# Layer 0: second products of two neighbouring routed tiles as one unit, four buffers for gated products, a new plan

## The reference

```python
def _swiglu(t, a, b, c):
    return jax.nn.silu(t @ a) * (t @ c) @ b
scores = jax.nn.softmax(xt @ gate_w.T, axis=-1)
topk_w, topk_i = jax.lax.top_k(scores, 2)
comb = jnp.zeros((T, E)).at[jnp.arange(T)[:, None], topk_i].add(topk_w)
for e in range(E):
    y = y + comb[:, e:e + 1] * _swiglu(xt, w1[e], w2[e], w3[e])
y + _swiglu(x, sw1, sw2, sw3)
```

## Time and profile before

| | us |
|---|---|
| median of 3 runs | 1134.03 |
| lowest and highest | 1131.99, 1137.25 |
| the profiled execution | 1132.48 |
| its span | 1130.3 |
| PE busy in it | 1026.9 |
| DVE busy | 869.8 |
| ACT busy | 730.9 |

### The profile page before, as it was taken

The page is one execution under the profiler, slowest core; times in us unless marked ns, Lnnn a source line. Parts: engine busy times, 40 slices in busy tenths (PEclk is TensorE's granted clock), DMA queues, the critical chain, the costliest instruction groups (busy, mean ns, idle before and its releaser), DMA issues.

```text
span 1130.3 us, 22735 instructions
## 1 busy us (share of the span) xinstructions
PE 1026.9 (91%) x8315; PEld 533.1 (47%) x8315; DVE 869.8 (77%) x1814; ACT 730.9 (65%) x1220; POOL 429.5 (38%) x484
## 2 busy tenths in 40 slices
PE   4589999889989999899889999899999889999996
PEld 2112222224555555446555566566565434455464
DVE  3799888898887888797557877777876688687455
ACT  4048766877767776666466566565657767767763
POOL 3000212354033346325135433453344468434463
PEclk9569988999999999999898999999999999999998
DMA  4804434356664777557548577695767846412110
GB/s 136 173 24 129 112 87 114 112 189 180 214 203 149 235 205 215 155 161 201 152 139 230 155 226 232 192 249 179 229 185 220 222 126 183 104 43 61 50 40 19
DMA packets 122510, 176.06 MB, mean 156 GB/s; under 512 B 20280, under 2 KB 86200, under 8 KB 122400
## 3 DMA queue, kind: packets, MB, share of 16 engines
q1 hardware_dynamic: 116064, 161.24, 49.1%
q0 software_dynamic: 5760, 12.59, 3.9%
q10 hardware_dynamic: 576, 0.79, 0.3%
HBM read 114.77 MB, written 59.67 MB: 154 GB/s over the span
## 4 chain that ended last, share of the span: by engine, by line
PE 46%; DVE 20%; DMA 15%; issue 8%; ACT 4%; POOL 3%; SPq 3%; POOLq 0%; DVEq 0%; ACTq 0%
DVE nm L965 12%; PE ps L775 10%; PE ps L837 8%; PE ps L758 5%; PE ps L736 5%; PE ps L856 5%; DMA gr<-d_y,pos 4%; PE ps L873 2%; PE ps L880 2%; DMA DR<-d_r 2%; ACT ES L1320 2%; DMA d_h<-r,pos 2%; PE ps L785 2%; DMA d_r<-DC 1%; PE ps L718 1%
## 5 line engine op out<-in xcount | busy, mean ns | idle before, releaser
L965 DVE TENSOR_REDUCE nm<-ps 128x2 f32<-128x1024 f32 (+3 forms) x512 | 507.7, 1016 | 103.5 <-PE ps L742 57.2
L1320 ACT ACTIVATE ES<-ps 128x1024 f32<-128x1024 f32 (+3 forms) x512 | 430.0, 862 | 160.3 <-PE ps L758 90.1
L775 PE MATMUL ps<-ES,VS 128*9 128x512 f32 (+3 forms) x2048 | 231.1, 528 | 0.8 <-DVE nmp L976 0.4
L736 PE MATMUL ps<-KS,QS 48*128 48x512 bf16 (+3 forms) x1024 | 183.8, 366 | 38.5 <-DVE nm L965 23.6
L758 PE MATMUL ps<-QS,KS 51*128 51x512 bf16 (+3 forms) x1024 | 178.0, 352 | 20.0 <-DVE nm L965 11.6
L837 PE MATMUL ps<-hsT,wst 128*128 128x128 f32 x1104 | 158.6, 288 | 3.7 <-DVE hdx L1158 3.4
L837 PEld LDWEIGHTS ps<-hsT,wst 128*128 128x128 f32 x1104 | 136.9, 194 | 38.6 <-issue 30.1
L758 PEld LDWEIGHTS ps<-QS,KS 51*128 51x128 bf16 x1024 | 49.6, 94 | 173.7 <-DVE nm L965 55.2
L736 PEld LDWEIGHTS ps<-KS,QS 48*128 48x128 bf16 x1024 | 50.0, 95 | 153.6 <-DVE nm L965 59.3
L1528 POOL DMA_INDIRECT gr<-d_y,pos x80 | 83.2, 1040 | 99.4 <-DMA gr<-d_y,pos 63.5
L856 PE MATMUL ps<-wst,hdx 128*128 128x128 f32 x552 | 84.7, 291 | 0.6 <-ACT hsT L1347 0.4
(11 more groups left out here) (196 smaller groups left out, 1405.4 us busy)
## 6 DMA issues: line engine op xcount, KB each, us to landing
wst<-we SPq DMA_DIRECT2D x92, 576.0 KB, 5.1
d_u<-US SPq DMA_DIRECT2D x64, 256.0 KB, 2.7
KS<-d_k SPq DMA_DIRECT2D x64, 192.0 KB, 4.8
QS<-d_q SPq DMA_DIRECT2D x64, 192.0 KB, 5.5
hs<-d_h SPq DMA_DIRECT2D x25, 256.0 KB, 4.0
d_y<-ys SPq DMA_DIRECT2D x25, 256.0 KB, 4.7
d_q<-sp SPq DMA_DIRECT2D x16, 384.0 KB
d_k<-sp SPq DMA_DIRECT2D x16, 384.0 KB, 3.4
```

Of the source, the lines that this page charges most:

```text
L736: mm = eng.matmul(psum[:, bank[u][a], 0:n], QS[m][r:r + KA, pr, 128 * t:128 * t + 128], KS[m][r:r + KA, pr, 0:n], start=True, stop=i < NB)
L775: mm = eng.matmul(psum[32 * a:32 * a + 9, b, q0:S], VS[i % 3][:, j, 4 * g + a, :], ES[(2 * (NT * (NG * i + g) + j) + a // 2) % NES][:, a % ...
L965: eng.tensor_reduce(nm[f][:, :].rearrange("p (a c) -> p a c", a=2)[:, :, 4 * pr + t], ps2("score", i, f, pr, t)[:, :, 0:n], AX.X, ALU.max, ...
L1320: eng.activation(ES[(2 * n + pp) % NES][:, :, 0:S - q0], ps2("bscore", i, f, g, j, pp)[:, :, 0:S - q0], ACT.Exp, scale=SC1 if i >= NB else ...
```

## The change

The second products of tiles 2m and 2m+1 of a group are one unit `x_dn`, under the odd tile's name; the 23rd tile of a group stays alone. It waits for both `x_mul`, opens one PSUM bank, writes the tiles' results side by side into 256 columns, and one `x_y` copies both. `hdx` has four buffers in place of two; the new two lie in `r1`, whose load therefore waits for the last `x_dn` of layer 0. What waited for a tile's `x_dn` now waits for its pair's: `x_gate` for the pair of the fourth tile before, `x_w` likewise. Both tiles of a pair are tied to the same place beside the scores. `c_ks` is put behind the second stack. In the planner the costs of nearly all PE units and some others are new, the lag of PE, DVE, ACT and POOL is 0.05 smaller, a change to full mode costs 0.2 instead of 0.1 and counts twice when units are chosen, and all rows of the NUDGE table are new (one is shown). Every engine's order changes with it.

```diff
-    "f": [0.01, 0.01, -0.1, 0.01, 0.06, -0.01, 0.0, 0.11, -1.15, -1.33, 0.44, -0.55, -0.34, -1.93, -2.64, -3.12],
+    "f": [0.07, -1.17, -0.89, -0.84, 0.0, 0.04, -0.07, -0.44, -3.9, -5.38, -2.53, -3.1, 0.27, -2.54, -4.21, -0.59],
...
-    LAG = {"PE": 0.48, "DVE": 0.31, "ACT": 0.33, "POOL": 0.25, "SP": 1.8}
+    LAG = {"PE": 0.43, "DVE": 0.26, "ACT": 0.28, "POOL": 0.2, "SP": 1.8}
...
-                    sw = 0.1 if e == "PE" and m != mode and w else 0.0
+                    sw = (0.2 if m == "full" else 0.1) if e == "PE" and m != mode and w else 0.0
...
-                t, sw, urg, k = min((f for f in fit if f[0] <= t0 + SLACK), key=lambda f: f[2] + SWITCH * (f[1] > 0))
+                t, sw, urg, k = min((f for f in fit if f[0] <= t0 + SLACK), key=lambda f: f[2] + SWITCH * (2 if f[1] > 0.15 else f[1] > 0))
...
+def pair(q, j):
+
+    return (q, min(j | 1, MT[q] - 1)) if q >= 0 and LAYER[q] == 0 else (q, j)
...
-        add("SP", ("c_ks", m), 0.8, 0.1 + 0.1 * m, [("c_one",)], lag=2.5)
+        add("SP", ("c_ks", m), 0.8, 0.1 + 0.1 * m, [("c_one",), ("stack", 0, 1)], lag=2.5)
...
-    load("r1", 6.0, 8.0, after=[("score", 6, 0, 0, 0)])
+    load("r1", 9.5, 8.0, after=[("x_dn",) + LAST0])
...
-            add("PE", ("p_proj", i, n), 0.95, u, [x] + ready, opens=1)
+            add("PE", ("p_proj", i, n), 0.86, u, [x] + ready, opens=1)
...
-                add("PE", ("pv", i, g, j), 0.12 + 0.86 * n / 512, u + 0.06, exps[-2:] + [("p_vs", i)] + ([("pv", i, g, j - 1)] if j else []), mode="cols", opens=int(j == 0))
+                add("PE", ("pv", i, g, j), 0.008 + 0.857 * n / 512, u + 0.06, exps[-2:] + [("p_vs", i)] + ([("pv", i, g, j - 1)] if j else []), mode="cols", opens=int(j == 0))
...
-                    k2 = back(k, 2, UNITS, UNIT)
-                    add("SP", ("x_w",) + k, 0.5, u - WEARLY, [("x_reg", q, h), ("x_dn",) + back(k, NST, UNITS, UNIT)], lag=3.6)
-                    beside = i + SPREAD[0] + SPREAD[1] * j / MT[q]
+                    k2, k4 = back(k, 2, UNITS, UNIT), pair(*back(k, 4, UNITS, UNIT))
+                    add("SP", ("x_w",) + k, 0.5, u - WEARLY, [("x_reg", q, h), ("x_dn",) + k4], lag=3.6)
+                    beside = i + SPREAD[0] + SPREAD[1] * (j // 2 * 2) / MT[q]
                     v = int(32 * (beside % 1))
                     for c in range(2):
-                        add("PE", ("x_up",) + k + (c,), 0.68, u, [("x_hst", q, L), ("x_w",) + k, ("x_dn",) + k2]
+                        add("PE", ("x_up",) + k + (c,), 0.68, u, [("x_hst", q, L), ("x_w",) + k, ("x_dn",) + k4]
                             + [("score", int(beside), v // 16, v // 4 % 4, v % 4)], opens=1)
                     add("ACT", ("x_th",) + k, 0.39, u, [("x_up",) + k + (0,), ("x_gate",) + k2])
-                    add("DVE", ("x_gate",) + k, 0.45, u, [("x_th",) + k, ("x_dn",) + k2], closes=[("x_up",) + k + (0,)])
+                    add("DVE", ("x_gate",) + k, 0.45, u, [("x_th",) + k, ("x_dn",) + k4], closes=[("x_up",) + k + (0,)])
                     add("DVE", ("x_mul",) + k, 0.45, u, [("x_gate",) + k, ("x_up",) + k + (1,)], closes=[("x_up",) + k + (1,)])
-                    add("PE", ("x_dn",) + k, 0.68, u, [("x_mul",) + k, ("x_st",) + l2], opens=1)
-                    add("ACT", ("x_y",) + k, 0.16, u, [("x_dn",) + k, ("m_st", 0), ("x_st",) + l2], closes=[("x_dn",) + k])
+                    if k == pair(*k):
+                        two = [(q, m) for m in range(j // 2 * 2, j + 1)]
+                        add("PE", ("x_dn",) + k, 0.67 * len(two), u, [("x_mul",) + m for m in two] + [("x_st",) + l2], opens=1)
+                        add("ACT", ("x_y",) + k, 0.05 + 0.11 * len(two), u, [("x_dn",) + k, ("m_st", 0), ("x_st",) + l2], closes=[("x_dn",) + k])
...
-        hdx = [sb(f"hdx{i}", [128, 384]) for i in range(2)]
+        hdx = [sb(f"hdx{i}", [128, 384])[:, :] for i in range(2)]
+
+        hdx += [r1[:, 3 * i:3 * i + 3, :].rearrange("p a b -> p (a b)") for i in range(2)]
...
-                    w = wst[fetched[p, j][0]]
-                    q.wait_ge(*on("x_mul", p, j))
-                    open_banks(u)
-                    for n in range(3):
-                        mm = eng.matmul(ps(*u)[:, 0:128], hdx[UNIT[p, j] % 2][:, 128 * n:128 * n + 128],
-                                        w[:, 2, 128 * n:128 * n + 128], start=(n == 0), stop=(n == 2))
+                    two = range(j // 2 * 2, j + 1)
+                    for t in two:
+                        q.wait_ge(*on("x_mul", p, t))
+                    open_banks(u)
+                    for t in two:
+                        w = wst[fetched[p, t][0]]
+                        for n in range(3):
+                            mm = eng.matmul(ps(*u)[:, 128 * (t % 2):128 * (t % 2) + 128], hdx[UNIT[p, t] % 4][:, 128 * n:128 * n + 128],
+                                            w[:, 2, 128 * n:128 * n + 128], start=(n == 0), stop=(n == 2))
...
-                    if p or j > 1:
-                        q.wait_ge(*on("x_dn", *back((p, j), 2, UNITS, UNIT)))
+                    if UNIT[p, j] >= 4:
+                        q.wait_ge(*on("x_dn", *pair(*back((p, j), 4, UNITS, UNIT))))
...
-                    L, n = (u[2] // 4, 1) if LAYER[p] == 0 else (u[2], min(4, MT[p] - 4 * u[2]))
-                    m, t0 = LOAD[p, L], u[2] % 4 if LAYER[p] == 0 else 0
+                    L, n = (u[2] // 4, u[2] % 2 + 1) if LAYER[p] == 0 else (u[2], min(4, MT[p] - 4 * u[2]))
+                    m, t0 = LOAD[p, L], u[2] % 4 // 2 * 2 if LAYER[p] == 0 else 0
...
+                    if u[1] == "r1":
+                        q.wait_ge(*on("x_dn", *LAST0))
...
-                        q.wait_ge(*on("x_dn", *back((p, j), NST, UNITS, UNIT)))
+                        q.wait_ge(*on("x_dn", *pair(*back((p, j), NST, UNITS, UNIT))))
...
```

More of the change, by code:

```diff
@@ L80 @@
 NUDGE = {
[L81 to L84, removed]
[9 rows of a table removed]
+    "p": [-1.09, 0.79, 2.64, -0.36, 0.63, 0.13, -0.14, -0.36, -0.4, 0.0, 0.0, 0.22, 0.0, -0.02, -0.64, -1.0],
+    "score": [-0.01, -0.05, -0.01, 0.0, 0.0, 0.0, 0.0, -0.04, 0.0, 0.0, 0.0, -0.06, -0.02, -0.02, 0.08, 0.45],
+    "max": [-0.46, -0.33, 0.11, 0.2, -0.22, -0.5, 0.08, -0.95, -0.07, -0.03, -1.83, -0.1, -0.84, -0.49, -5.11, 1.19],
+    "expo": [-0.04, -0.01, 0.0, 0.0, 0.0, 0.0, 0.0, 0.0, 0.0, 0.0, -0.04, -0.23, -0.01, -0.03, 0.19, -0.33],
[9 rows of a table added]
 }
@@ L317, in plan @@
             u = i + 0.85 + 0.5 * f
-            add("PE", ("max_turn", i, f), 0.2, u, [done[-1]], opens=1)
+            add("PE", ("max_turn", i, f), 0.11, u, [done[-1]], opens=1)
             add("ACT", ("max_hi", i, f), 0.16, u, [("max_turn", i, f), ("max_st", i - 1, f)])
@@ L347, in plan @@
         add("DVE", ("t_o", i), 0.61, u, [("t_ld", i)])
-        add("PE", ("t_mm", i), 0.95, u, [("t_o", i), ("ld", "bo"), after_t(i - 1)], opens=1)
+        add("PE", ("t_mm", i), 0.9, u, [("t_o", i), ("ld", "bo"), after_t(i - 1)], opens=1)
         add("DVE", ("t_add", i), 0.61, u, [("t_mm", i), ("ld", "bo"), after_t(i - 1)], closes=[("t_mm", i)])
@@ L388, in plan @@
             add("DVE", ("rr_oh", q), 0.2, u, [("r_keep", first + c) for c in range(size)])
-            add("PE", ("rr_mm", q), 0.4, u, [("rr_oh", q), ("c_more", 1)], opens=1)
-            add("DVE", ("rr_a", q), 1.25, u, [("rr_mm", q)], closes=[("rr_mm", q)])
-            add("DVE", ("rr_pos", q), 3.8, u, [("rr_a", q)] + ([("g_ga", GROUPS[q - 1][0] - 1, t, c) for t in range(NT) for c in range(2)] if q > 1 else []))
-            add("DVE", ("rr_tex", q), 1.2, u, [("rr_pos", q)] + ([("x_reg", q - 2, (MT[q - 2] - 1) // 12)] if q > 1 else []))
+            add("PE", ("rr_mm", q), 0.07, u, [("rr_oh", q), ("c_more", 1)], opens=1)
+            add("DVE", ("rr_a", q), 0.8 + 0.08 * size, u, [("rr_mm", q)], closes=[("rr_mm", q)])
+            add("DVE", ("rr_pos", q), 3.2 + 0.2 * size, u, [("rr_a", q)] + ([("g_ga", GROUPS[q - 1][0] - 1, t, c) for t in range(NT) for c in range(2)] if q > 1 else []))
+            add("DVE", ("rr_tex", q), 0.7 + 0.13 * size, u, [("rr_pos", q)] + ([("x_reg", q - 2, (MT[q - 2] - 1) // 12)] if q > 1 else []))
             sent = [("rr_pos", q)] * 4
@@ L443, in plan @@
                     for k in range(2):
-                        add("POOL", ("g_ga", i0, t, k), 1.28, u, [("x_st", q, L) for L in range(XL[q])] + [sent[-2], ("g_w", i0 - 1, t)], lag=2.1)
+                        add("POOL", ("g_ga", i0, t, k), 1.35, u, [("x_st", q, L) for L in range(XL[q])] + [sent[-2], ("g_w", i0 - 1, t)], lag=2.1)
                         sent.append(("g_ga", i0, t, k))
@@ L1153, in _ @@
                     p, j = u[1:]
-                    m = UNIT[p, j] % 2
+                    m = UNIT[p, j] % 4
                     q.wait_ge(*on("x_th", p, j))
-                    if p or j > 1:
-                        q.wait_ge(*on("x_dn", *back((p, j), 2, UNITS, UNIT)))
-                    eng.scalar_tensor_tensor(out=hdx[m][:, :], in0=tx[m][:, :], scalar=1.0, in1=ps("x_up", p, j, 0)[:, 0:384],
```

(3 more changed lines are left out.)

16 lines of the change are left out of this document (8 added, 8 removed), and 16 rows, old and new, of the table NUDGE.

## The result

The changed kernel takes 1147.45 us (median of 4 runs, 1144.03 to 1152.42), the kernel before 1133.01 on the same chip (4 runs, 1130.24 to 1137.25): a ratio of 1.0144, 95% interval 1.0104 to 1.0184. It is 14 us slower, where 11 us faster was forecast, and it lies outside the range of 1102 to 1139. Lines of this profile are those of before plus 9 on TensorE up to L847, and plus 12 on its later lines and on DVE, ACT and POOL.

A forecast was written before the change was run, and what follows sets the result against it. TensorE was taken to bound the long middle (95.6% busy from 282.5 to 847.5 us). Gains of 4.7 + 1 + 5.0 = 10.7 us off 1132.5 gave 1121.8, taken as 1122; 8-in-10 range 1102 to 1139.

The forecast's parts named there:

- (1): Layer 0 second products on TensorE: 92 units become 48, saving mode switches; 4.7 us gain, bounds 0 and 12.3.
- (2): ScalarE's copies of second products: 92 become 48, 7.4 us of ACT work goes, but it is covered; value 0.
- (3): Four `hdx` buffers let a pair's gates and first products run ahead; 1 us gain, bounds 0 and 3.4.
- (4): Expert weight loads wait for a pair; the 5.1 us fetch is hidden by the 12.7 us pair interval; value 0.
- stores of SP behind a waiting `x_w`: On SP's queue: stores of projections, sums and maxima stand behind a waiting weight load; no size given.
- weights come late: Slower rival: bunched pairs make TensorE wait for weight fetches, 39 us less 10.7, about 1161 us; chance 0.07.
- (5): New planner costs and due times: 26 fewer full-array stretches, 5.0 us gain; idle time change 0 within -8 and +8.
- (6): `c_ks` loads moved later on SP, near the first projection stores; gain between 0 and 5.68 us, value 0.
- (7): Load of `r1` moved to near 850, covered by some 70 us; value 0, loss up to 10.0 if `d_up` came forward.
- the middle ended later though TensorE was busy less: Sign of a wrong prediction, for the stretch from 282.5 to 847.5 us; slower outcomes together had chance 0.16.
- PE waiting for weights: Sign of a wrong prediction: TensorE waits for the expert weights, which don't exist in the kernel before.
- the new order starves scoring: Slower rival: longer full-array runs leave DVE without a score, 0.5 us at 50 runs, 1147 us; chance 0.09.

The follow-up runs named there:

- e6: Kernel before in its written-down order, weights freed in pairs, second products merged at the odd tile's place, banks handed out anew; 1146.91 us, ratio 1.0111.
- e7: Changed kernel in its order on every engine, each pair split back into two adjacent units with two copies, banks handed out anew; 1141.66 us.
- e11: Kernel before in its written-down order, single second products, weight buffers freed only with the pair's second tile, banks handed out anew; 1144.50 us, ratio 1.0109.
- e14: Kernel before in its order, every layer 0 weight load issued at the next one's place, banks handed out anew; 1136.52 us, ratio 1.0042.

## Why the prediction was wrong

- **(1) Merge, 4.7 us: the count was right, the worth was not.** 48 units, 552 passes. Of full-array stretches the merge alone takes 11 (325 to 314, e6); the 40 fewer are mostly the order's. But e7 is not slower than the changed kernel (1141.66 and 1147.45), and e6 against e11 puts the merge at +2. So the term is nearer its lower bound, 0, than 4.7, and a small loss isn't excluded.
- **(2) Copies: right.** 7.5 us of ACT work went (28.8 to 21.3; forecast 7.4), and nothing came of it.
- **(3) Four buffers: small, and misread.** The wait of 3.4 us is gone, but it was TensorE waiting for the bank that a late `x_gate` frees, and the gate stood behind a gather that DVE waited 4.5 us for, at 589. No buffer of `hdx` was in it, and e11, with two buffers, has 1.3 us there.
- **(4) Weights freed in pairs, value 0: this step failed.** Its argument was that a fetch of 5.1 us is hidden by 12.7 us of pair interval, and that only waits of first products on weights would tell. In the changed kernel there are none, nor in e11, so that argument held. But e11, which has this part and the banks that go with it, costs 12 us (ratio 1.0048 to 1.0169), near the whole loss. The step looked only at the reader of the load, and 0 followed for the whole part. It left out who else moves when the loads do: what lands beside a gather that DVE waits for in order (3.93 us near 744), and which unit frees the bank of the next (3.14 us at 610). How the rest of the 12 us comes about stays open. The path that the prediction named beside it, stores of SP behind a waiting `x_w`, doesn't grow: SP waits 88.1 us for second products in e11 and 132.0 in before. The rival "weights come late" had the right part and the wrong path; its price of 39 less 10.7 was twice too high.
- **(5) Reorder, 5.0 us and "0 within -8 and +8" for the idle time: this failed too.** The stretches fell by 40, not 26, and TensorE's busy time by 8.1 us, near the forecast of 8 (which was for the middle). But the idle rose by 20. Once pairs are in (e6, 1146.91), the new order with its fewer stretches (285 against 314 in e6) brings nothing: 1147.45. Its 5 us don't show, and no run shows that it causes the loss.
- **(6), (7): not tested apart.** The first score starts at 30.69 us instead of 33.62, but by 39 us 0.4 is left of that: 0, as forecast. The load of `r1` goes out at 883.9, its first reader runs at 931.4 and doesn't wait for it; the cover is 47 us, not 70.

The sum by measurement, all from medians: freeing in pairs with its banks +12, merging about +2, new order and the rest about 0; it was forecast as 0, -5 and -6. These intervals overlap, so the 12 and the 2 are not sharp.

One sign in the prediction's own list held: the middle ended later though TensorE was busy less. It was named as a way to fail and then given a chance of only 0.16 together with the rest. The other named sign, PE waiting for weights, was the wrong place to look. The rival "the new order starves scoring" gave 1147 us, and 1147.45 was measured, but that is luck: DVE's waits for scores ahead of rowmax (L965, L977 now) fell from 100.8 to 89.5 us.

**Open.** Why paired release costs 12 us and a load that is a tile late 4. The rows show one stall worth 5 us in e11, which e6 lacks, and one of 3 us through the banks; the rest is waits under 2 us. A run with paired release and the banks of before kept would settle the share of the banks; it was not made. Six weight buffers instead of four, with which a load would not wait for its pair as long, were not tried. Whether the changed kernel's loss and e11's come from the same places was not shown, only that they are equal in size. No version faster than the kernel before was found.

## What to carry to other kernels

When buffers are freed in groups, don't put the price at 0 because the fetch is hidden from its own reader: list every other transfer in flight then and what is queued behind its reader (an advice from one stall, not a shown cause of the 12 us). To price a part of a scheduled kernel, write its order down, buffers and banks with it, and change that part alone; refitting the schedule moves the time by more (4 us for a shaken table, 27 to 39 for a mismatched one) than the part is worth. Saved busy time of the bound engine (8.1 us here) is no gain until its idle time is seen not to grow.

## What the runs showed of the hardware

**A stall costs more than its length.** In e11 TensorE waits 5.34 us; the granted clock is 0.70 in 740 to 744 and 0.50, the level of 1.2 GHz, in 744 to 748 (rows above), when it works again. A unit of 12 first-product passes then holds the engine from 746.85 to 749.04, 2.19 us, where before takes 745.25 to 746.69, 1.44. e14's wait of 3.19 us at the same place leaves the clock at 1.00 in every stretch from 742 to 752. The changed kernel behind its wait of 4.18 us:

```profile
384.21 1.09 PE L694 MATMUL ps<-ident,xn 128*128 128x128 f32 x4 [4.18 <-ACT US L1339]
```

```profile
384.00:388.00 4.00, 3.79 (x19) 2.73 (x19) 0.80 (x2) 2.65 (x5) 2.38 (x3) 0.57 0.31 102
```

**A small DVE operation waits inside itself.** The addition on L988 takes 0.28 us in the median; its mean is 431 ns in the changed kernel (316 before). In one place it stretches while POOL adds two tiles. DVE's and POOL's timelines of the changed kernel:

```profile
856.22 2.92 DVE L988 TENSOR_TENSOR nmp<-rj,nmp 32x128 bf16<-32x128 f32 x1
...
856.72 2.27 POOL L1477 TENSOR_TENSOR sp<-sr,sp 128x512 bf16<-128x512 f32 x2
```

It ends at 859.14, just behind POOL's 858.99. The Trainium skill (SBUF — State Buffer, Terms) says that DVE and GpSimd arbitrate for a shared port pair and that the loser fully blocks for the whole instruction. The trace agrees in the end of the wait; that DVE's row starts 0.50 us ahead of POOL's additions, beside a scatter of POOL's, and lasts through both of them, goes beyond it. DVE is busy 882.0 us in the changed kernel against 869.8 with the same 1814 instructions, so an order can lengthen the work as well as the waits. Of the 12.2 us, 6.5 are on this line and the cast ahead of it (L985): 9 of their 64 instructions take over 0.4 us beside an addition of POOL's, and 2 before. Where the other 5.7 come from was not traced.
